# First attention, second set of eight heads: exponentials read PSUM one head at a time, with the negated row maximum as bias, and 1/4 goes into the head mask

## The chip, the cores and the metric

The kernel runs on one core of a Trainium2 chip. A time is the device time of one execution, in microseconds (us), lower being better. The core has five engines with queues of their own: TensorE (PE, with its weight loads PEld), VectorE (DVE), ScalarE (ACT), GpSimd (POOL) and SyncE (SP, which here only starts transfers).

## The reference

A two-layer network on x of 16 batches x 128 tokens x 256 features: cross attention, a quantised FFN, an mLSTM-like attention, and a mixture of eight experts. The change lies in the first part:

```python
qp = q @ Wq                       # q: layer norm of x
kp, vp = split(kv @ Wkv)          # kv: the context
# 16 heads of 16 features, scale = 16 ** -0.5 = 1/4
dots = jnp.einsum('bhid,bhjd->bhij', qh, kh) * scale
attn = jax.nn.softmax(dots, axis=-1)
out = jnp.einsum('bhij,bhjd->bhid', attn, vh)
x = x + out.reshape(B, N, D) @ Wout
```

## The kernel before

Each engine has a program of its own, written out by hand, and they meet at semaphores: `x.then_inc(s, 1)` raises s when x is done, `engine.wait_ge(s, n)` holds the engine's queue until s is n. Each queue runs strictly in its order.

The first attention handles one batch (128 tokens, 16 heads) per step, 16 steps, b = 0 to 15. The heads are worked in two sets of eight, m = 0 and 1; the scores of a set, 128 x 1024 fp32, fill two PSUM banks, `S_ps[m]`. In a step, for each set:

- TensorE makes the scores (`scores`, L698). A query tile of 32 features holds two heads; GpSimd has multiplied the keys with a 0/1 mask, `pair_mask`, so that each head meets only its own features (`mask_k`, L522, into `kbd`).
- VectorE takes the maximum over each row of each head (L1304, into `row_max`) and subtracts it from all of the scores, PSUM to SBUF (L1306, into `probs`): `softmax_shift`.
- ScalarE takes the exponential of `probs` in place, 1024 columns in one instruction, with 1/4 as scale (L1033): `exps`.
- TensorE transposes the eight heads back into the same PSUM banks (`probs_transposes`, L705); ScalarE copies them to SBUF (`probsT_copy`, L1041); TensorE multiplies with the values (`values`, L718), which carry a column of ones, so that the sum of the exponentials comes out beside them.

Between these, the engines work on the step before (`tail_a` L725, `tail_norm` L1313 and L1315, `tail_b` L731, ScalarE's copy L1058, `tail_c` L737, the output product, and VectorE's `tail_add`, L1320 and on) and on the step after (`front_transposes`, `front_products` L682 and L687, ScalarE's copies L1025, L1029, L1037). TensorE's order in a step is:

```python
scores(b, p, 0); values(b - 1, 1 - p, 1); front_transposes(b + 1, ...)
scores(b, p, 1); tail_a(b - 1); front_products(b + 1, ...); tail_b(b - 1)
probs_transposes(b, 0); tail_c(b - 1); probs_transposes(b, 1); values(b, p, 0)
```

ScalarE's order: outT_copy, front, `exps(b, 0)`, qk_copy, v_copy, the copy of L1058, `exps(b, 1)`, probsT_copy twice. VectorE's order: softmax_shift(b, 0), norm, tail_norm, softmax_shift(b, 1), tail_add; and in the last seven steps a piece of the FFN's weight preparation behind that (`late`: gate_up_maxima in step 9, then weight_scales, down_rounded, gate_up_scaled, gate_up_shifted, gate_up_rounded, early_norms).

Before the loop VectorE takes the statistics of the 16 batches in groups of four (L1271 to L1275), GpSimd raises each group to -1/2 (L513), and only behind the fourth does GpSimd's queue come to the first mask products. `pair_mask` itself is made by VectorE after the first group, from `head_mask`.

Of the kernel before, what the change touches and what calls it, by code (L numbers as in the profile page):

```python
# [8 lines left out]
def build(nc, x, ctx_in, wq, wkv, wout, clip_x, clip_down, w_gate, w_up, w_down, ig_k, ig_b, fg_k, fg_b, rms_scale,  # L9
# [5 lines left out]
    ALU = mybir.AluOpType  # L15
    ACT = mybir.ActivationFunctionType
    AX = mybir.AxisListType

    B, S, D = x.shape
    P = 128  # L20
    KT = D // P
    H0 = 16
    DH0 = D // H0
    HT = P // DH0
# [27 lines left out]
    with stack:  # L52
        def sb(name, shape, dt=F32):
            return stack.enter_context(nc.sbuf_tensor(name, shape, dt))
# [4 lines left out]
        def sem(name):  # L59
            return stack.enter_context(nc.semaphore(name))  # L60
# [24 lines left out]
        pair_mask = sb("pair_mask", [P, 2])  # L85
# [112 lines left out]
        def bank(n, *shape, count=1, dt=F32):  # L198
            view = psum[:, n, :] if count == 1 else psum[:, n:n + count, :].rearrange("p n c -> p (n c)")
            if dt != F32:  # L200
                view = view.bitcast(dt)
            names = "abcde"[:len(shape)]
            return view.rearrange(f"p ({' '.join(names)}) -> p {' '.join(names)}", **dict(zip(names[1:], shape[1:])))
# [4 lines left out]
        S_ps = [bank(3, HT, P, count=2), bank(5, HT, P, count=2)]  # L208
# [7 lines left out]
        consts_ready = sem("consts_ready")  # L216
# [13 lines left out]
        max_ready = sem("max_ready")  # L230
        shifted_ready = sem("shifted_ready")
        probs_ready = sem("probs_ready")
# [257 lines left out]
        def _(pool):  # L490
# [25 lines left out]
            def mask_k(b, p, inner=False):  # L516
                pool.wait_ge(qk_evac, b + 1)
                if inner or b >= 2:

                    pool.wait_ge(s_done, 2 * (b - 2) + 2)  # L520
                for m in range(KT):
                    nc.gpsimd.tensor_tensor(kbd[:, p, m, :, :],  # L522
                                            qkT[:, p, KT + m, :].unsqueeze(1).to_broadcast([P, 2, P]),
                                            pair_mask[:].unsqueeze(2).to_broadcast([P, 2, P]),
                                            ALU.mult).then_inc(kbd_ready, 1)
# [2 lines left out]
            nc.gpsimd.memset(one_col[:], 1.0).then_inc(fw_preset, 1)  # L528
            nc.gpsimd.tensor_copy(ident_b[:], ident[:]).then_inc(fw_preset, 1)

            pool.wait_ge(consts_ready, 7)
            mask_k(0, 0)
            mask_k(1, 1)
            with pool.Fori(0, (B - 2) // 2) as i:
# [485 lines left out]
        def _(act):  # L1020
            act_fn = nc.scalar.activation
# [7 lines left out]
                act_fn(qkT[:, p, :, :], bank1[:, :, :], ACT.Copy).then_inc(qk_evac, 1)  # L1029

            def exps(b, m):
                act.wait_ge(shifted_ready, 2 * b + m + 1)
                act_fn(probs[:, m, :, :], probs[:, m, :, :], ACT.Exp, scale=float(DH0) ** -0.5).then_inc(probs_ready, 1)  # L1033

            def v_copy(b, p):
                act.wait_ge(v_done, b + 1)
# [39 lines left out]
            for q in range(3):  # L1076
                last = act_fn(wguT[:, :, 4 * q:4 * q + 4, :].rearrange("p k n c -> p n k c"), bank(q, 4, KT, P, dt=BF16), ACT.Copy)
# [190 lines left out]
        def _(dve):  # L1268
            def row_stats(b, chain):

                nc.vector.bn_stats(stats[:, 0, :], x_sb[:, b, :]).then_inc(ln_chain, 1)  # L1271
                dve.wait_ge(ln_chain, chain + 1)
                nc.vector.bn_aggr(mv[:, b, :], stats[:, 0, :]).then_inc(ln_chain, 1)
                dve.wait_ge(ln_chain, chain + 2)
                nc.vector.tensor_scalar_add(rstd[:, b:b + 1], mv[:, b, 1:2], LN_EPS).then_inc(ln_chain, 1)  # L1275

            def norm(b, p, inner=False):
                if inner or b >= 2:

                    dve.wait_ge(t1_done, b - 1)  # L1280
                nc.vector.tensor_scalar(xn[:, p, :], x_sb[:, b, :], mv[:, b, 0:1], rstd[:, bass.ds(b, 1)] if inner else rstd[:, b:b + 1],
                                        ALU.subtract, ALU.mult).then_inc(xn_ready, 1)
# [6 lines left out]
            for i in range(4):  # L1289
                dve.wait_ge(x_loaded[i], 16)  # L1290
                for b in range(4 * i, 4 * i + 4):
                    row_stats(b, 3 * b)
                if i == 0:
                    dve.wait_ge(rstd1_ready, 1)
                    norm(0, 0)
                    norm(1, 1)
                    dve.wait_ge(consts_ready, 6)
                    nc.vector.tensor_reduce(pair_mask[:], head_mask[:].rearrange("p (g r) -> p r g", r=2), AX.X,
                                            ALU.add).then_inc(consts_ready, 1)
            dve.wait_ge(rstd1_ready, 4)  # L1300

            def softmax_shift(b, m):
                dve.wait_ge(s_done, 2 * b + m + 1)
                nc.vector.tensor_reduce(row_max[:, m, :], S_ps[m][:, :, :], AX.X, ALU.max).then_inc(max_ready, 1)  # L1304
                dve.wait_ge(max_ready, 2 * b + m + 1)
                nc.vector.tensor_tensor(probs[:, m, :, :], S_ps[m][:, :, :],  # L1306
                                        row_max[:, m, :].unsqueeze(2).to_broadcast([P, HT, P]),
                                        ALU.subtract).then_inc(shifted_ready, 1)

            def tail_norm(b):  # L1310
                dve.wait_ge(to_done, b + 1)
# [247 lines left out]
            for n in range(2):  # L1559
                last = nc.vector.tensor_scalar(gates8[0:R, n, :], gates8[0:R, n, :], gbias[0:R, n:n + 1], None, ALU.add)  # L1560
# [289 lines left out]
```

## Time and profile before

| | |
|---|---|
| three runs | 877.24, 881.13, 881.49 us, median 881.13 |
| the profiled execution | 880.42 us, its span 878.7 us |
| busy over the span | PE 686.7, PEld 473.8, DVE 545.8, ACT 394.6, POOL 248.4 us |
| granted TensorE clock, mean | 0.867 |
| subtractions of L1306 | 32, 1224 ns each |
| maxima of L1304 | 32, 1219 ns each |
| exponentials of L1033 | 32, 1057 ns each |

The span goes from the first to the last instruction; the time of the execution has 1.7 us around it. Busy time is that of each engine alone, over all stages; the first attention takes some 180 us of the span, and only its rows bear on the change. The granted clock is a share of TensorE's full speed, 1.00 being the higher level and 0.50 the lower.

### The profile page before, as it was taken

The page shows a single profiled execution, that of the slowest core. Times are in us where ns is not written, and L with a number is a line of the kernel's source. Part 1 is how long each engine was busy: PE and PEld are TensorE (multiplying, and loading weights), DVE is VectorE, ACT ScalarE, POOL GpSimd, SP SyncE. Part 2 cuts the span into 40 slices and gives each one's busy share as a digit, 9 for nine tenths or more (in the row PEclk, how much of TensorE's full clock was granted, in tenths as well). Part 3 has the DMA queues.
Part 4 walks back from the last instruction along what each step waited for, and adds up shares of the span by engine and source line. Part 5 has one row for each costly group of instructions (what it writes and reads, how often), then busy time and mean ns, then how long its engine had stood idle before and what let it go on. Part 6 is the DMA issues. An engine that isn't in the chain of part 4 may idle for free.

```text
span 878.7 us, 19300 instructions
## 1 busy us (share of the span) xinstructions
PE 686.7 (78%) x4567; PEld 473.8 (54%) x4611; DVE 545.8 (62%) x1394; ACT 394.6 (45%) x811; POOL 248.4 (28%) x372
## 2 busy tenths in 40 slices
PE   3999999983745695277616989898989989889992
PEld 2778877761223473266513556565655655556661
DVE  5577789974989654398785464555455455564440
ACT  1466655544633254355314453535444545453330
POOL 3111111110000200644402353545344272653421
PEclk9799999985985598555556999999999999999996
DMA  8100000000000111511172433343251515431113
GB/s 256 31 13 14 15 12 12 0 1 0 1 0 0 31 54 30 211 31 30 41 248 66 127 73 87 104 125 73 37 160 24 167 30 166 127 72 24 30 25 108
DMA packets 45843, 58.41 MB, mean 66 GB/s; under 512 B 13496, under 2 KB 39416, under 8 KB 45272
## 3 DMA queue, kind: packets, MB, share of 16 engines
q1 hardware_dynamic: 38328, 47.79, 16.7%
q0 software_dynamic: 7488, 10.31, 7.4%
q8 instruction: 11, 0.18, 0.1%
q14 instruction: 16, 0.13, 0.0%
HBM read 145.90 MB, written 11.80 MB: 179 GB/s over the span
## 4 chain that ended last, share of the span: by engine, by line
PE 47%; DVE 20%; issue 15%; POOL 7%; DMA 3%; ACT 3%; DVEq 2%; ACTq 1%; POOLq 1%; SPq 0%
PE psum L962 16%; PE psum L984 7%; PE psum L698 3%; PE psum L975 3%; PE psum L682 3%; PE psum L705 2%; POOL region L638 2%; PE psum L862 2%; DVE region L1455 2%; PE psum L718 1%; PE psum L737 1%; DMA region<-xrow_dram,next_token 1%; PE psum L687 1%; PE psum L855 1%; POOL region L561 1%
## 5 line engine op out<-in xcount | busy, mean ns | idle before, releaser
L962 PE MATMUL psum<-region 128*128 x897 | 209.3, 381 | 18.9 <-issue 6.0
L962 PEld LDWEIGHTS psum<-region 128*128 128x128 bf16 x936 | 91.7, 98 | 117.8 <-issue 28.6
L984 PE MATMUL psum<-region 128*128 x936 | 113.9, 280 | 6.3 <-DVE region L1799 3.7
L984 PEld LDWEIGHTS psum<-region 128*128 128x128 bf16 x936 | 92.1, 100 | 23.1 <-issue 9.7
L1769 DVE TENSOR_TENSOR region<-psum,region 128x512 f32<-128x512 f32 x78 | 53.9, 691 | 72.8 <-ACT region L1209 63.5
L1209 ACT ACTIVATE region<-psum 128x512 f32<-128x512 f32 x78 | 46.5, 597 | 116.6 <-PE psum L962 108.2
L620 POOL DMA_INDIRECT sum_dram<-region,tok_idx x39 | 62.0, 1589 | 6.9 <-issue 6.6
L608 POOL TENSOR_TENSOR pause_p<-minus_half 128x1 f32<-128x1 f32 x37 | 7.1, 193 | 192.3 <-DVE next_token L1785 191.6
L1230 ACT ACTIVATE pause_a<-one_col 128x1 f32<-128x1 f32 x117 | 23.7, 202 | 83.9 <-issue 68.8
L1799 DVE TENSOR_TENSOR region<-psum,region 128x1024 bf16<-128x1024 f32 x39 | 47.7, 1222 | 19.1 <-ACT region L1217 19.1
L522 POOL TENSOR_TENSOR region<-region,pair_mask 128x256 f32<-128x256 f32 x32 | 18.9, 613 | 138.3 <-ACT region L1029 138.3
L609 POOL DMA_INDIRECT region<-xrow_dram,next_token x39 | 41.0, 1052 | 39.6 <-DVE next_token L1764 27.4
L1749 DVE MEMSET pause_d<- 128x1 f32 x80 | 4.7, 59 | 73.4 <-ACT pause_a L1233 39.1
L1304 DVE TENSOR_REDUCE region<-psum 128x8 f32<-128x1024 f32 x32 | 39.0, 1219 | 14.6 <-PE psum L698 14.5
L1217 ACT ACTIVATE region<-psum 128x1024 bf16<-128x1024 f32 x39 | 39.9, 1023 | 16.0 <-PE psum L975 15.0
L1232 ACT ACTIVATE region<-region 128x2048 f32 x24 | 45.8, 1909 | 0.0
L895 PE MATMUL psum<-region 128*128 128x96 f32 x128 | 32.0, 433 | 17.6 <-DVE region L1579 8.8
L1033 ACT ACTIVATE region<-region 128x1024 f32<-128x1024 f32 x32 | 33.8, 1057 | 25.8 <-DVE region L1306 25.8
L1751 DVE TENSOR_TENSOR region<-region 128x2048 f32 x17 | 39.0, 2294 | 2.6 <-issue 2.6
L698 PE MATMUL psum<-region 32*128 32x256 f32 x256 | 38.1, 417 | 3.0 <-POOL region L522 3.0
L975 PEld LDWEIGHTS psum<-ident,region 128*128 128x128 f32 x312 | 36.5, 141 | 7.4
L975 PE MATMUL psum<-ident,region 128*128 128x128 f32 x312 | 40.4, 273 | 0.0
(295 smaller groups left out, 1362.6 us busy)
## 6 DMA issues: line engine op xcount, KB each, us to landing
region<-in_L_ffn_w SPq DMA_DIRECT2D x117, 1024.0 KB
region<-in_ctx SPq DMA_DIRECT2D x48, 128.0 KB, 2.1
region<-neg_max_dram SPq DMA_DIRECT2D x4, 1024.0 KB, 7.6
xrow_dram<-region SPq DMA_DIRECT2D x1, 2080.0 KB, 7.8
x_sb<-in_x SPq DMA_DIRECT2D x4, 512.0 KB, 6.6
sum_dram<-x_sb SPq DMA_DIRECT2D x1, 2048.0 KB, 7.5
region<-in_L_ffn_w_down SPq DMA_DIRECT2D x1, 704.0 KB, 8.3
region<-in_L_ffn_w_gate SPq DMA_DIRECT2D x1, 640.0 KB, 8.9
```

Of the source, the lines that this page charges most:

```text
L609: pool.indirect_dma_start(xg[:, p, :], None, xrow_dram, bass.IndirectOffsetOnAxis(ap=next_token[:, p:p + 1], axis=0)).then_inc(xg_loaded[p ...
L620: pool.indirect_dma_start(sum_dram, bass.IndirectOffsetOnAxis(ap=tok_idx[:, p:p + 1], axis=0), y_d[:, p, :], None, compute_op=ALU.add).the ...
L698: last = mm(S_ps[s][:, 4 * r + 2 * m:4 * r + 2 * m + 2, :], qkT[rows, p, m, :], kbd[rows, p, m, :, :], start=True, stop=True)
L962: last = mm(psum[:, 2 * f + n, :], (xT_lo if xl else xT_hi)[:, p, k, :], weights_at(place, wl, n, k * F1 + f * FH, FH), start=(i == 0), st ...
L975: last = tr(bank(4, F1 // P, P, count=2)[:, f, :], h_d[:, p, f * P:(f + 1) * P], ident[:])
L984: last = mm(psum[:, 7, 0:D], (hT_lo if hl else hT_hi)[:, f, :], weights_at(place, wl, 2, f * D, D), start=(i == 0), stop=(i == 3 * (F1 // ...
L1209: act_fn(sil_d[:, f, :], psum[:, 2 * f, :], ACT.Silu).then_inc(sil_d_ready, 1)
L1217: act_fn(hT_hi, bank(4, F1 // P, P, count=2), ACT.Copy).then_inc(hT_high, 1)
L1232: act_fn(expert_w[:, bass.ds(place + n * PART, PART)], stage[:, p, n, :], ACT.Copy)
L1304: nc.vector.tensor_reduce(row_max[:, m, :], S_ps[m][:, :, :], AX.X, ALU.max).then_inc(max_ready, 1)
L1769: tt(h_d[:, p, f * FH:(f + 1) * FH], psum[:, 2 * f + 1, :], sil_d[:, f, :], ALU.mult).then_inc(h_d_ready, 1)
L1799: tt(hT_lo, bank(4, F1 // P, P, count=2), hT_hi, ALU.subtract).then_inc(hT_low, 1)
```

## The change

For the second set of heads (m = 1) the subtraction on VectorE is gone. The maximum is written negated, and ScalarE waits for it and takes eight exponentials of 128 columns, one per head, that read the scores in PSUM and take that head's negated maximum as bias. The first set keeps subtraction (now an addition of the negated maximum) and its one exponential. The scale 1/4 leaves the exponentials: `pair_mask` is multiplied with it once, so that the scores come out scaled; that multiply raises `consts_ready` to 8, for which GpSimd now waits.

```diff
--- before.py
+++ after.py
@@ -528,7 +528,7 @@
             nc.gpsimd.memset(one_col[:], 1.0).then_inc(fw_preset, 1)
             nc.gpsimd.tensor_copy(ident_b[:], ident[:]).then_inc(fw_preset, 1)
 
-            pool.wait_ge(consts_ready, 7)
+            pool.wait_ge(consts_ready, 8)
             mask_k(0, 0)
             mask_k(1, 1)
             with pool.Fori(0, (B - 2) // 2) as i:
@@ -1029,8 +1029,14 @@
                 act_fn(qkT[:, p, :, :], bank1[:, :, :], ACT.Copy).then_inc(qk_evac, 1)
 
             def exps(b, m):
-                act.wait_ge(shifted_ready, 2 * b + m + 1)
-                act_fn(probs[:, m, :, :], probs[:, m, :, :], ACT.Exp, scale=float(DH0) ** -0.5).then_inc(probs_ready, 1)
+                if m == 0:
+                    act.wait_ge(shifted_ready, b + 1)
+                    act_fn(probs[:, m, :, :], probs[:, m, :, :], ACT.Exp).then_inc(probs_ready, 1)
+                else:
+                    act.wait_ge(max_ready, 2 * b + 2)
+                    for h in range(HT):
+                        last = act_fn(probs[:, m, h, :], S_ps[m][:, h, :], ACT.Exp, bias=row_max[:, m, h:h + 1])
+                    last.then_inc(probs_ready, 1)
 
             def v_copy(b, p):
                 act.wait_ge(v_done, b + 1)
@@ -1297,15 +1303,18 @@
                     dve.wait_ge(consts_ready, 6)
                     nc.vector.tensor_reduce(pair_mask[:], head_mask[:].rearrange("p (g r) -> p r g", r=2), AX.X,
                                             ALU.add).then_inc(consts_ready, 1)
+                    dve.wait_ge(consts_ready, 7)
+                    nc.vector.tensor_scalar_mul(pair_mask[:], pair_mask[:], float(DH0) ** -0.5).then_inc(consts_ready, 1)
             dve.wait_ge(rstd1_ready, 4)
 
             def softmax_shift(b, m):
                 dve.wait_ge(s_done, 2 * b + m + 1)
-                nc.vector.tensor_reduce(row_max[:, m, :], S_ps[m][:, :, :], AX.X, ALU.max).then_inc(max_ready, 1)
-                dve.wait_ge(max_ready, 2 * b + m + 1)
-                nc.vector.tensor_tensor(probs[:, m, :, :], S_ps[m][:, :, :],
-                                        row_max[:, m, :].unsqueeze(2).to_broadcast([P, HT, P]),
-                                        ALU.subtract).then_inc(shifted_ready, 1)
+                nc.vector.tensor_reduce(row_max[:, m, :], S_ps[m][:, :, :], AX.X, ALU.max, negate=True).then_inc(max_ready, 1)
+                if m == 0:
+                    dve.wait_ge(max_ready, 2 * b + 1)
+                    nc.vector.tensor_tensor(probs[:, m, :, :], S_ps[m][:, :, :],
+                                            row_max[:, m, :].unsqueeze(2).to_broadcast([P, HT, P]),
+                                            ALU.add).then_inc(shifted_ready, 1)
 
             def tail_norm(b):
                 dve.wait_ge(to_done, b + 1)
```

ScalarE's instructions of one step inside the loop, in the order of its queue, first as they were (from the copy L1045 that opens the step):

```order
L1045 ACTIVATE region<-psum 128x512
L1024 REGISTER_ALU
L1025 ACTIVATE region<-psum 128x512
L1032 ISA
L1033 ACTIVATE region<-region 128x1024
L1029 ACTIVATE region<-psum 128x512
L1037 ACTIVATE region<-psum 128x16x16
L1058 ACTIVATE region<-psum 128x256
L1032 REGISTER_ALU
L1033 ACTIVATE region<-region 128x1024
L1041 ACTIVATE region<-psum 128x1024 x2
```

and with the change (line numbers shift; L1034 is the exponential of set 0, L1038 those of set 1, L1064 the copy before them):

```order
L1051 ACTIVATE region<-psum 128x512
L1024 REGISTER_ALU
L1025 ACTIVATE region<-psum 128x512
L1033 REGISTER_ALU
L1034 ACTIVATE region<-region 128x1024
L1029 ACTIVATE region<-psum 128x512
L1043 ACTIVATE region<-psum 128x16x16
L1063 REGISTER_ALU
L1064 ACTIVATE region<-psum 128x256
L1036 ISA
L1038 ACTIVATE region<-psum,region 128x128 x8
```

In the place of one 128x1024 activation on SBUF stand eight of 128x128 that read PSUM; nothing else of the step has moved.

VectorE's instructions in the middle of the same step, from the maximum of set 0 to the residual add, as they were:

```order
L1303 ISA
L1304 TENSOR_REDUCE region<-psum 128x8
L1306 TENSOR_TENSOR region<-psum,region 128x1024
L1281 ISA x2
L1281 TENSOR_SCALAR region<-x_sb,mv,rstd 128x256
L1313 RECIPROCAL region<-psum 128x16
L1315 TENSOR_TENSOR region<-psum,region 128x256
L1303 REGISTER_ALU
L1304 TENSOR_REDUCE region<-psum 128x8
L1306 TENSOR_TENSOR region<-psum,region 128x1024
L1320 ISA
L1320 TENSOR_TENSOR x_sb<-x_sb,psum 128x256
```

and with the change:

```order
L1311 ISA
L1312 TENSOR_REDUCE region<-psum 128x8
L1315 TENSOR_TENSOR region<-psum,region 128x1024
L1287 ISA x2
L1287 TENSOR_SCALAR region<-x_sb,mv,rstd 128x256
L1322 RECIPROCAL region<-psum 128x16
L1324 TENSOR_TENSOR region<-psum,region 128x256
L1311 REGISTER_ALU
L1312 TENSOR_REDUCE region<-psum 128x8
L1329 ISA
L1329 TENSOR_TENSOR x_sb<-x_sb,psum 128x256
```

The second TENSOR_TENSOR of 128x1024 is gone, and the residual add (L1329, before L1320) follows the second maximum directly.

## Rows read from the trace of the kernel before

**Rows 1.** The windows view: busy us and instructions of each engine, TensorE clock, transfers.

```profile
63.00:73.00 10.00, 10.00 (x101) 8.17 (x100) 7.69 (x16) 6.42 (x10) 1.18 (x2) 1.00 0.04 13
123.00:135.00 12.00, 10.15 (x97) 7.65 (x96) 11.65 (x23) 5.85 (x10) 1.18 (x2) 1.00 0.04 11
178.00:189.00 11.00, 8.42 (x75) 6.41 (x73) 9.28 (x18) 4.97 (x7) 2.27 (x1) 0.80 0.01 1
```

**Rows 2.** The chain that ended last, first attention: start us, us, what.

```profile
32.85 1.09 PE psum L705 x8
...
112.64 0.87 PE psum L705 x8
...
121.74 0.88 PE psum L737 x4
...
124.60 3.26 DVE w_amax L1363
```

**Rows 3.** Timeline of step 5: start us, us, engine, line, operation [idle before].

```profile
78.88 1.21 DVE L1304 TENSOR_REDUCE region<-psum 128x8 f32<-128x1024 f32 x1
...
80.13 1.23 DVE L1306 TENSOR_TENSOR region<-psum,region 128x1024 f32<-128x1024 f32 x1
...
81.18 0.38 ACT L1058 ACTIVATE region<-psum 128x256 f32<-128x256 f32 x1
81.44 1.06 ACT L1033 ACTIVATE region<-region 128x1024 f32<-128x1024 f32 x1
...
81.79 1.03 PE L737 MATMUL psum<-region 128*128 128x256 f32 x4
...
82.65 1.04 PE L705 MATMUL psum<-ident,region 128*128 128x128 f32 x8
...
83.62 0.65 PE L718 MATMUL psum<-region 128*32 128x128 f32 x16
```

**Rows 4.** ScalarE's groups by shape: count, busy us, mean ns, idle before.

```profile
L1033 ACT ACTIVATE region<-region 128x1024 f32<-128x1024 f32 x32 | 33.8, 1057 | 25.8 <-DVE region L1306 25.8
L1041 ACT ACTIVATE region<-psum 128x1024 f32<-128x1024 f32 x32 | 32.7, 1022 | 6.1 <-PE psum L705 6.1
...
L1105 ACT ACTIVATE sil<-psum,gu_scale 128x512 f32<-128x512 f32 x24 | 16.4, 686 | 12.8 <-DVE region L1455 12.8
...
L1158 ACT ACTIVATE region<-region 128x128 f32 x40 | 12.9, 390 | 2.0 <-issue 1.6
...
L1029 ACT ACTIVATE region<-psum 128x512 f32<-128x512 f32 x16 | 9.5, 594 | 20.2 <-PE psum L682 20.2
...
L1037 ACT ACTIVATE region<-psum 128x256 f32<-128x256 f32 x16 | 6.1, 383 | 4.5 <-PE psum L687 4.5
```

**Rows 5.** Timeline of ScalarE alone, in the later mLSTM stage.

```profile
385.50 0.37 ACT L1174 ACTIVATE region<-psum 128x256 f32<-128x256 f32 x1
385.76 0.41 ACT L1175 ACTIVATE region<-region 128x256 f32 x1
...
386.37 1.28 ACT L1158 ACTIVATE region<-region 128x128 f32 x4
```

**Rows 6.** Timeline of step 10.

```profile
131.11 1.21 DVE L1304 TENSOR_REDUCE region<-psum 128x8 f32<-128x1024 f32 x1
...
131.25 0.44 PE L731 MATMUL psum<-ident,region 128*128 128x128 f32 x2 [0.67 <-DVE region L1315]
...
132.36 1.23 DVE L1306 TENSOR_TENSOR region<-psum,region 128x1024 f32<-128x1024 f32 x1
...
133.62 1.06 ACT L1033 ACTIVATE region<-region 128x1024 f32<-128x1024 f32 x1 [1.25 <-DVE region L1306]
...
134.73 1.09 PE L705 MATMUL psum<-ident,region 128*128 128x128 f32 x8 [1.18 <-ACT region L1033]
```

**Rows 7.** Timeline of the start, GpSimd.

```profile
18.53 1.01 POOL L513 TENSOR_TENSOR rstd<-rstd,minus_half 128x4 f32<-128x4 f32 x1 [1.95 <-DVE rstd L1275]
```

**Rows 8.** Timeline of step 15, TensorE's output product.

```profile
187.55 1.91 PE L737 MATMUL psum<-region 128*128 128x256 f32 x4
```

## The prediction

> **What bounds the kernel now.** The change touches only the first attention, which runs from about 21 to 200 us of the span, so I read that stretch alone. First the windows [rows 1]: between 63 and 73 us TensorE is busy 10.00 us of 10 at clock 1.00, VectorE 7.69, ScalarE 6.42. Between 123 and 135 us it is VectorE that is full, 11.65 us of 12, and TensorE has gaps. So the sixteen steps of the loop have two regimes. The chain that ended last says where they part [rows 2]: the transposes of the second set of heads (L705) stand on it once per step from 32.85 us, in step 0, to 112.64 us, in step 8, that is nine times; from step 9 it leaves TensorE after the output product (L737, 121.74 us), takes VectorE's tail of the step and goes into the FFN weight preparation that is hung on the last seven steps (`late`), first the 3.26 us piece of w_amax at 124.60. I call steps 0 to 8 TensorE's steps and steps 9 to 15 VectorE's steps.
>
> Then the timeline of one TensorE step, step 5 [rows 3], which decides the case. The row maximum of set 1 is there from 78.88 + 1.21 = 80.09. VectorE subtracts it (80.13, 1.23 us). But ScalarE doesn't wait for that subtraction: it starts the exponentials at 81.44, right behind its two copies, and they end at 82.50. TensorE's second transposes start at 82.65, 0.86 us after the product before them (81.79), which is that product's own pace. So the exponentials of set 1 come out 0.1 us or so before TensorE wants them, and their start is set by ScalarE's queue, not by VectorE. Nothing there waits for the subtraction, and whatever lengthens the exponentials is paid by TensorE.
>
> **The change part by part.** (1) VectorE loses one 128x1024 subtraction (1.23 us) in each of 16 steps, 19.7 us of busy time. In the nine TensorE steps that is worth nothing, as just read. In the seven others it takes the place of a link that the exponentials have to wait for; see (3). The edits that cost nothing: `negate` on the maximum and the missing scale on the exponentials change no instruction's size; the 1/4 is in the mask, and the mask products (L522) keep their shape.
>
> (2) ScalarE's one exponential of 1024 columns (1.06 us, SBUF to SBUF) becomes eight of 128 columns that read PSUM and take a bias from SBUF. That form is not in the trace, so I bound it by its neighbours [rows 4]. A copy from PSUM takes 0.594 us for 512 columns and 0.383 for 256, so 128 take 0.383 - 0.106 = 0.277. An operand by pointer costs 0.686 - 0.594 = 0.09 (the silu of L1105, with its scale column, against the plain copy of 512 columns). Sum 0.367. The other way: the decays (L1158) are just this instruction but for SBUF as source, 0.390 us; PSUM as source is 0.035 faster (1.057 against 1.022 for 1024 columns), so 0.355. I take 0.36. What counts more is the distance from start to start in a run of them. Four decays in a row take 1.28 us [rows 5], (1.28 - 0.39) / 3 = 0.298 apart; less 0.035 for PSUM that is 0.263. A PSUM copy of 256 columns starts the next instruction 0.26 us later, for 0.37 of its own [rows 5], an overlap of 0.11, and 0.367 - 0.11 = 0.257. I take 0.26. Eight then take 7 x 0.26 + 0.36 = 2.18 us in place of 1.06.
>
> The high bound is the decays' own pace, 7 x 0.298 + 0.39 = 2.48 us. The low bound leaves the pointer free: 7 x (0.277 - 0.11) + 0.277 = 1.45 us. I stay near the high side since the decays are the nearest row.
>
> The Trainium skill, page "ScalarE: Activation LUTs", section "What ACT_TABLE_LOAD costs", gives an activation with a bias by pointer 280 ns + 0.833 ns a column, and an overlap of 93 ns back to back. By that rule eight would be 7 x 0.294 + 0.387 = 2.44 us, and the total below would be about +12.3 us instead of +9.9; the decays' rows agree with it (0.390 and 0.298), and it makes no difference for a source in PSUM, where the copies' rows do.
>
> In step 5 the exponentials start at 81.44 as before (the maximum was ready at 80.09, before ScalarE's copy of L1058 began at 81.18), and end at 83.62. Where TensorE has waited for them, its transposes start 0.05 us after their end and take 1.09 instead of 1.04 [rows 3, 6], so everything behind starts (83.62 + 0.05 + 0.05) - 82.65 = 1.07 us later. All that follows in the step hangs on those transposes or on ScalarE's copies behind the same exponentials (the values at 83.62), which keep their distance: ScalarE's probsT copy ends about 0.1 us before the eight transposes do, as now. The next step's exponentials start again behind TensorE's L687 and ScalarE's two copies, so nothing is caught up and the delay adds up: nine steps, 9 x 1.07 = 9.6 us; a step grows from 9.97 us (the first and the last L705 of [rows 2] are 79.79 us apart, over 8 steps) to 11.0.
>
> (3) VectorE's steps. In step 10 [rows 6] the maximum of set 1 ends at 132.32, the subtraction at 133.59, the exponential at 134.68, and TensorE waits until 134.73, idle meanwhile. With the change the eight exponentials can start at 132.36 and end at 134.54: -0.14 us. The subtraction that goes and the longer exponentials pay for each other, there and in steps 12, 13 and 15. VectorE isn't released sooner either: its next work there, the residual add, waits for TensorE's L737 (132.42 + 1.13 = 133.55), just when the subtraction ends now. In steps 9, 11 and 14 the exponentials are off the chain, because it goes from L737 through VectorE; but there TensorE starts the following step 1.07 us later and had only 0.5 to 0.7 us of idle before its next link with VectorE (0.67 in step 10 [rows 6]), so 0.3 to 0.4 us comes through. I put the seven steps at 0 in all, -1 to +1.
>
> (4) The start. VectorE gets a wait for its own mask reduction and a small multiply, about 0.2 us with the semaphore, ahead of twelve batches' statistics. GpSimd's fourth rsqrt waits for these, and the first mask product and first scores for that [rows 7]: +0.2 us. The new `consts_ready` count of 8 is long reached by then.
>
> **Sum.** 9.6 + 0 + 0.2 = +9.8. The later stages hold none of the changed lines. The profiled execution took 880.42 us (span 878.7); the three runs' median is 881.13, 0.7 above. 881.1 + 9.8 = 890.9, from the profiled execution 890.2.
>
> **Rivals.**
> A, forecast: the exponentials become TensorE's wait in nine steps. With the bounds of (2): run 2.48 gives 1.37 per step, +12.5; run 1.9 gives 0.79, +7.3; with +-1 for (3): 887 to 895. Chance 0.80.
>
> B, not slower: the pointer is hidden when the instructions stand back to back. Run 1.45: (1.45 - 1.11) = 0.34 per step, 3.1 + 0.2, less about 0.7 in each of steps 10, 13 and 15: +1.2, 882.3. Below a run of 1.11 us a TensorE step costs nothing, and that is where it turns; if the eight followed at the pace of their columns alone (7 x 0.106 + 0.36 = 1.10), VectorE's three steps would gain 1.2 us each: 877.7. For it: the first of the bounds is only argued. Against it: the decays, four in a row, show 0.298 and not 0.106. Chance 0.07, of which 0.02 for a gain over 0.5%.
>
> C, the clock: TensorE now idles 1.1 us in nine more steps. At the end of this stage, where VectorE kept it waiting, the granted clock is 0.80 over a stretch [rows 1], the lower level (1.2 GHz) for part of it, and the product of L737, 1.03 us in step 5, took 1.91 [rows 3, 8]. If it fell for some 7 to 10 us in the loop, 3 to 5 us would come on top: 895 to 897. Against it: in 123 to 135 us TensorE was idle 1.85 us and the clock stayed at 1.00 [rows 1], at its higher level (2.4 GHz). Chance 0.08.
>
> D, more hangs on the second set than I see: the eight reads of PSUM slow beside TensorE's transposes into the other banks, or the run is no better than one duration each, 8 x 0.37 = 2.96. Then 1.85 per step: +17, 898. Chance 0.05.
>
> **The numbers.** Likeliest 890.9. The range goes from the low side of A, with a little of B, to the low side of C, with the other stages' scatter of +-2 us that the three runs show: 885.5 to 896.5. A measurement of this kernel tells about 0.5%, 4.4 us, from no change. Faster 0.02 and within it 0.08 are B and the lowest end of A; slower 0.90.
>
> **What would show it.** In the profile after: eight exponentials, 0.36 us each, taking about 2.2 us together; TensorE's L705 waiting some 1.1 us for them in steps 0 to 8, step length 11.0; VectorE's busy time down by some 19.5 us and the span up all the same; the first scores 0.2 us later; clock 1.00 through the loop. The forecast is wrong if the run takes under 1.6 us, or if a TensorE step doesn't stretch by what the run grew.

## The result, and the profile after

The changed kernel is slower: median 892.81 us of four runs against 880.10 of the kernel before, ratio 1.0142, 95% interval 1.0105 to 1.0178. Timed a second time, as the last of the experiments, it took 890.17 against 879.26, ratio 1.0133 (1.0114 to 1.0152). The forecast was 890.9 with a range of 885.5 to 896.5. The profiled execution took 889.77 us, span 888.0.

From the page of the changed kernel, busy time by engine and the granted clock in 40 slices:

```profile
PE 678.4 (76%) x4567; PEld 466.2 (52%) x4611; DVE 527.3 (59%) x1379; ACT 412.1 (46%) x923; POOL 251.0 (28%) x372
...
PEclk9899999997997599555555999999999999999997
```

VectorE is busy 18.5 us less than before (545.8), ScalarE 17.5 us more (394.6), and the span is 9.3 us longer. The load moved from one engine to the other, almost one for one; below it turns out that only the second one counts. What the two instructions became, in the groups of ScalarE and of VectorE (the latter for 20 to 215 us):

```profile
L1038 ACT ACTIVATE region<-psum,region 128x128 f32<-128x128 f32 x128 | 34.8, 396 | 0.2 <-DVE region L1312 0.2
L1047 ACT ACTIVATE region<-psum 128x1024 f32<-128x1024 f32 x32 | 33.8, 1057 | 4.3 <-PE psum L705 4.3
```

```profile
L1312 DVE TENSOR_REDUCE region<-psum 128x8 f32<-128x1024 f32 x32 | 39.0, 1218 | 24.1 <-PE psum L698 24.0
L1315 DVE TENSOR_TENSOR region<-psum,region 128x1024 f32<-128x1024 f32 x16 | 19.6, 1224 | 0.5
```

L1038 is the new line, 128 times, 0.396 us each; L1047, the copy of the transposed heads, is L1041 of before; sixteen subtractions are left (L1315) of 32. The windows that answer to [rows 1], moved to the same work. The first starts with the residual add of step 3 and spans one step, 11.0 us now; the second starts 0.36 us behind the residual add of step 9, as 123.00 did before:

```profile
65.51:76.51 11.00, 10.15 (x98) 8.05 (x98) 6.47 (x14) 7.46 (x17) 1.18 (x2) 1.00 0.04 12
131.91:143.91 12.00, 10.57 (x102) 8.48 (x103) 10.37 (x22) 8.22 (x19) 1.18 (x2) 1.00 0.03 11
```

In a TensorE step VectorE has fallen from 7.69 to 6.47 us, by one subtraction. TensorE was busy 10.00 us of ten and is busy 10.15 of eleven: it now waits. Its clock stays at 1.00. In the stretch of step 9 to 10, where VectorE was full (11.65 of 12), it is busy 10.37 of 12, and TensorE isn't full either (10.57). The timeline of step 5 shows the wait; the columns are those of [rows 3]:

```profile
83.52 1.21 DVE L1312 TENSOR_REDUCE region<-psum 128x8 f32<-128x1024 f32 x1
...
85.82 0.38 ACT L1064 ACTIVATE region<-psum 128x256 f32<-128x256 f32 x1
86.08 2.17 ACT L1038 ACTIVATE region<-psum,region 128x128 f32<-128x128 f32 x8
...
86.43 1.03 PE L737 MATMUL psum<-region 128*128 128x256 f32 x4
87.60 0.42 DVE L1329 TENSOR_TENSOR x_sb<-x_sb,psum 128x256 f32 x1 [2.88 <-PE psum L737]
...
88.07 1.09 ACT L1047 ACTIVATE region<-psum 128x1024 f32<-128x1024 f32 x1
...
88.31 1.09 PE L705 MATMUL psum<-ident,region 128*128 128x128 f32 x8 [0.85 <-ACT region L1038]
...
89.33 0.65 PE L718 MATMUL psum<-region 128*32 128x128 f32 x16
```

The maximum is ready at 84.73, ScalarE's copy L1064 starts at 85.82, and the eight exponentials start at 86.08, 0.26 us behind it, just as the one of 1024 columns did. They take 2.17 us where that took 1.06. TensorE's product L737 starts at 86.43; its transposes could follow 0.86 us later, at 87.29, and start at 88.31, 0.06 us behind the exponentials. VectorE meanwhile idles 2.88 us before the residual add L1329. ScalarE's copy of the transposed heads (L1047), which starts right behind the run, shows 1.09 instead of 1.02 us, and the values (L718) follow 1.02 us after L705's start, where it was 0.97 [rows 3]: the 0.05 us that the forecast had counted for transposes that had to wait. The chain that ended last now has the exponentials on it in each of the first nine steps:

```profile
33.23 1.09 PE psum L705 x8
...
42.03 2.15 ACT region L1038 x8
...
121.33 1.09 PE psum L705 x8
...
130.64 0.88 PE psum L737 x4
...
133.50 3.26 DVE w_amax L1372
...
141.53 1.92 ACT region L1038 x7
143.49 1.09 PE psum L705 x8
```

Compare [rows 2]: there the transposes followed TensorE's own product. Now each L705 stands behind some 2.16 us of L1038. From 130.64 to 133.50 the chain goes through VectorE as before, and comes back through L1038 at 141.53. That is step 10, the counterpart of [rows 6]:

```profile
140.01 1.21 DVE L1312 TENSOR_REDUCE region<-psum 128x8 f32<-128x1024 f32 x1
...
141.26 2.17 ACT L1038 ACTIVATE region<-psum,region 128x128 f32<-128x128 f32 x8
...
141.48 1.03 PE L737 MATMUL psum<-region 128*128 128x256 f32 x4
142.54 0.42 DVE L1329 TENSOR_TENSOR x_sb<-x_sb,psum 128x256 f32<-128x256 f32 x1 [1.32 <-PE psum L737]
```

The exponentials start at 141.26, 0.04 us behind the maximum, and end at 143.43: 2.21 us after the maximum, where subtraction and exponential took 2.36. VectorE, spared its subtraction, idles 1.32 us for L737.

Starts of VectorE's residual add, one per step, give the length of each step without reading anything else. The first one stands in step 1, ahead of that step's second transposes, so the first distance holds what step 1 pays, and the fifteenth what step 15 pays. The fifteen distances, in us:

| kernel | first eight | ninth to thirteenth | fourteenth, fifteenth |
|---|---|---|---|
| before | 9.93 to 9.98, 9.85 at the end; sum 79.49 | 10.95, 11.36, 10.81, 11.35, 10.93 | 11.46, 9.28 |
| changed | 10.99 to 11.05, 10.92 at the end; sum 88.03 | 10.99, 11.16, 11.00, 11.04, 11.11 | 9.74, 9.28 |

Eight steps give 8.54 us, 1.07 each. The next five are 55.40 and 55.30. The 11.46 of the kernel before is not its softmax: the clock stood at its lower level from 184.6 to 191.4 us in that execution, and in other profiles of the same steps it did or didn't (below), so 1.7 us of the real difference are hidden in this pair of profiles.

### The profile page after: what moved, and what is told of

Same layout as the page of the kernel before. It is cut to its first block, busy times and chain, and to the rows that moved or that the text cites. A ratio compares the mean times of both kernels' runs of the same rounds, so it can differ in the third digit from the quotient of the medians.

```text
span 888.0 us, 19411 instructions
## 1 busy us (share of the span) xinstructions
PE 678.4 (76%) x4567; PEld 466.2 (52%) x4611; DVE 527.3 (59%) x1379; ACT 412.1 (46%) x923; POOL 251.0 (28%) x372
## 4 chain that ended last, share of the span: by engine, by line
PE 44%; DVE 18%; issue 15%; POOL 8%; ACT 6%; DMA 3%; DVEq 2%; POOLq 1%; ACTq 1%; SPq 0%
PE psum L962 16%; PE psum L984 6%; PE psum L698 3%; POOL region L638 3%; ACT region L1038 3%; PE psum L682 3%; PE psum L975 3%; DVE region L1464 2%; PE psum L862 2%; PE psum L705 2%; PE psum L718 2%; PE psum L687 1%; PE psum L855 1%; POOL region L561 1%; POOL pause_p L636 1%
## 5 line engine op out<-in xcount | busy, mean ns | idle before, releaser
L962 PE MATMUL psum<-region 128*128 x897 | 210.3, 383 | 21.1 <-POOL pause_p L640 7.4
L962 PEld LDWEIGHTS psum<-region 128*128 128x128 bf16 x936 | 91.9, 98 | 120.6 <-issue 32.0
L984 PE MATMUL psum<-region 128*128 x936 | 109.1, 273 | 6.2 <-DVE region L1808 3.8
L984 PEld LDWEIGHTS psum<-region 128*128 128x128 bf16 x936 | 89.4, 98 | 21.0 <-issue 9.7
L705 PE MATMUL psum<-ident,region 128*128 128x128 f32 x256 | 34.1, 276 | 14.8 <-ACT region L1038 14.7
L975 PE MATMUL psum<-ident,region 128*128 128x128 f32 x312 | 40.4, 273 | 0.0
L975 PEld LDWEIGHTS psum<-ident,region 128*128 128x128 f32 x312 | 36.5, 141 | 7.4
L705 PEld LDWEIGHTS psum<-ident,region 128*128 128x128 f32 x256 | 28.2, 141 | 21.3 <-ACT region L1038 21.0
```

Source lines behind the costliest of these rows:

```text
L705: last = tr(S_ps[m][:, h, :], probs[:, m, h, :], ident[:])
L962: last = mm(psum[:, 2 * f + n, :], (xT_lo if xl else xT_hi)[:, p, k, :], weights_at(place, wl, n, k * F1 + f * FH, FH), start=(i == 0), st ...
L975: last = tr(bank(4, F1 // P, P, count=2)[:, f, :], h_d[:, p, f * P:(f + 1) * P], ident[:])
L984: last = mm(psum[:, 7, 0:D], (hT_lo if hl else hT_hi)[:, f, :], weights_at(place, wl, 2, f * D, D), start=(i == 0), stop=(i == 3 * (F1 // ...
```

## The experiments

Theory A is the forecast: ScalarE's queue stands before TensorE's second transposes, its eight exponentials take 1.1 us longer than the one, and nine steps pay. The rivals: M, the loss comes from the mask, the start or later stages; V, VectorE's relief is worth something that the loop's loss hides; and on the price, whether it is the cutting into eight, the pointer, or the work on ScalarE as such that costs. Ratios are to the kernel before, on the same chip each time.

### The mask alone

```diff
-                if m == 0:
-                    act.wait_ge(shifted_ready, b + 1)
...
-                        last = act_fn(probs[:, m, h, :], S_ps[m][:, h, :], ACT.Exp, bias=row_max[:, m, h:h + 1])
...
+                act.wait_ge(shifted_ready, 2 * b + m + 1)
+                act_fn(probs[:, m, :, :], probs[:, m, :, :], ACT.Exp).then_inc(probs_ready, 1)
```

and the subtraction for both sets; the 1/4 stays in the mask.

> Only the mask part of the change: 1/4 in the head mask, negated maxima, but both sets keep VectorE's subtraction and the one exponential of 1024 columns. If the loss is TensorE's wait for the eight exponentials (theory A), this is as fast as before, the start aside: 0 to +0.3 us in the attention, ratio 0.998 to 1.003 to the kernel before. If the loss came from the start, the mask or from later stages that merely run in another phase (rival M), it would show here: +3 us or more.

Measured 880.37 against 879.45, ratio 1.0013 (0.9999 to 1.0027). Its timeline, ScalarE in step 6:

```profile
90.56 0.38 ACT L1058 ACTIVATE region<-psum 128x256 f32<-128x256 f32 x1
90.83 1.06 ACT L1033 ACTIVATE region<-region 128x1024 f32<-128x1024 f32 x1
91.78 1.02 ACT L1041 ACTIVATE region<-psum 128x1024 f32<-128x1024 f32 x1
```

The exponential starts 0.27 us behind the copy and takes 1.06 us, as before; the first eight steps sum to 79.47 us, then 10.95, 11.36, 10.80, 11.35, 10.94, 9.75, 9.28. The mask and the start cost about 1 us by the medians, between nothing and 2.4 us by the interval. This kernel is also the better base for comparing steps, its profile having no lower clock in the last two distances: against it the changed kernel's fifteen distances sum to 162.35 - 153.90 = +8.45 us.

### Eight exponentials, SBUF to SBUF, without a bias

```diff
-                act_fn(probs[:, m, :, :], probs[:, m, :, :], ACT.Exp)
+                    for h in range(HT):
+                        last = act_fn(probs[:, m, h, :], probs[:, m, h, :], ACT.Exp)
```

for m = 1, on top of the mask-only kernel.

> As the mask-only kernel, but the exponential of set 1 is cut into eight of 128 columns, SBUF to SBUF, behind VectorE's subtraction, without a bias by pointer. Theory A with the pointer as most of the price: starts 0.2 us apart (0.298 less 0.09), a run of about 1.7 us, TensorE 0.6 us late per step in nine steps, in all +5 to +6 us; VectorE's steps are longer too, since the subtraction stays. If it is the cutting itself that costs (the pointer being free), the run is as long as with bias, some 2.2 to 2.4 us, and the kernel +10 us or more.

Measured ratio 1.0112 (1.0063 to 1.0161), 888.79 against 879.45 or +9.3 us, more than the +5 to +6 expected. The group of the eight, then step 5 in the timeline:

```profile
L1037 ACT ACTIVATE region<-region 128x128 f32<-128x128 f32 x128 | 27.2, 302 | 4.0 <-DVE region L1313 4.0
```

```profile
84.53 1.70 ACT L1037 ACTIVATE region<-region 128x128 f32<-128x128 f32 x8
...
86.28 1.09 PE L705 MATMUL psum<-ident,region 128*128 128x128 f32 x8 [0.37 <-ACT region L1037]
```

The run takes 1.70 us, just as expected, and steps are 10.52 us, +0.59. That makes 4.7 us in eight steps. The last seven sum to 4.2 us more than in the mask-only kernel. There the exponentials still stand behind the subtraction, and in steps 10, 12 and 15 both are on the chain: steps of 12.03 and 13.54 us are among them (11.36 and 11.35 there). The clock has a part in it that isn't told apart here: it stood at its lower level from 163.8 to 167.2 us, in the second of these steps, and from 194.5 to 201.3, in the last two. The expectation had put too little on these seven.

### Eight exponentials from PSUM, without a bias

```diff
-                        last = act_fn(probs[:, m, h, :], S_ps[m][:, h, :], ACT.Exp, bias=row_max[:, m, h:h + 1])
+                        last = act_fn(probs[:, m, h, :], S_ps[m][:, h, :], ACT.Exp)
```

> The changed kernel with the bias left out of the eight exponentials of set 1: they still wait for the maximum and read PSUM, but nothing is subtracted, so the guard against large scores is missing in that set. Theory A with the pointer price: starts about 0.17 apart, run 1.45 us, TensorE 0.35 us late per step, +3 us over before in the loop and about -1 in VectorE's steps: +1 to +3 us. If the pointer is free back to back, the run stays at 2.17 us and the kernel at +9 to +13.

Measured ratio 1.0044 (1.0027 to 1.0062), 884.02 against 879.45, +4.6 us: the run and the step came out as expected, the whole above the +1 to +3. Its fifteen distances sum to 2.9 us more than those of the mask-only kernel, with the clock at its lower level from 187.2 to 190.6 us in one of them; the rest isn't traced.

```profile
L1038 ACT ACTIVATE region<-psum 128x128 f32<-128x128 f32 x128 | 23.5, 325 | 0.2 <-DVE region L1312 0.2
```

```profile
93.52 1.48 ACT L1038 ACTIVATE region<-psum 128x128 f32<-128x128 f32 x8
...
95.05 1.09 PE L705 MATMUL psum<-ident,region 128*128 128x128 f32 x8 [0.15 <-ACT region L1038]
```

A run of 1.48 us (1.45 expected), steps of 10.30 to 10.41 (10.23 at the end), +0.37. With these two the price of the pieces is measured: starts are (1.48 - 0.325) / 7 = 0.165 us apart from PSUM without a pointer, (1.70 - 0.302) / 7 = 0.200 from SBUF, and (2.17 - 0.396) / 7 = 0.253 from PSUM with the bias by pointer. And TensorE's delay follows the run with one constant:

| set 1's exponentials | run, us | step, us | step over 9.93 | run less 1.11 |
|---|---|---|---|---|
| one of 1024, from SBUF | 1.06 | 9.93 | 0 | below 0 |
| eight, PSUM, no bias | 1.48 | 10.30 | 0.37 | 0.37 |
| eight, SBUF, no bias | 1.70 | 10.52 | 0.59 | 0.59 |
| eight, PSUM, bias | 2.17 | 11.00 | 1.07 | 1.06 |

### The change in steps 9 to 15 only, and in steps 0 to 8 only

```diff
+                new = isinstance(b, int) and b >= 9
-                if m == 0:
+                if m == 0 or not new:
```

with the same condition in VectorE's softmax_shift, and, for the other kernel, the opposite condition in both. Both programs' loops cover steps 1 to 8, and steps 9 to 15 are written out.

> The change made in steps 9 to 15 alone, where VectorE is the bound; steps 0 to 8 keep subtraction and one exponential for set 1 (1/4 in the mask throughout). Theory A: the seven steps come out at 0, -1 to +1 us; ratio 0.998 to 1.002. Rival V (VectorE's relief is real there and the loop's loss was larger than it looks): -2 us or more. If the exponentials cost in every step alike, +7 us.

Measured ratio 1.0004 (0.9987 to 1.0021). Steps 9.93 to 9.98, then 11.00, 11.16, 11.00, 11.04, 11.11, 9.74, 9.29: the changed kernel's last seven behind the old kernel's first nine.

> The counterpart of the kernel with the change in steps 9 to 15 alone: the change in steps 0 to 8, and subtraction plus one exponential for set 1 in steps 9 to 15. Theory A: the whole loss is here, nine steps of 1.09 us, 9.8 us, of which the whole changed kernel keeps all: +9 to +13 us, ratio 1.010 to 1.014, like the whole change. A rival in which the two halves act on each other (the later steps' relief pays back part) would make this slower than the whole change by 2 us or more.

Measured ratio 1.0103 (1.0075 to 1.0131), 884.89 against 875.73, +9.2 us. Steps of 11.0, then 10.95, 11.37, 10.79, 11.36, 10.93. The loss is in the first nine steps, all of it; rival V falls, for the last seven give nothing back by themselves.

### One exponential from PSUM, without a bias

```diff
-                    for h in range(HT):
-                        last = act_fn(probs[:, m, h, :], S_ps[m][:, h, :], ACT.Exp, bias=row_max[:, m, h:h + 1])
-                    last.then_inc(probs_ready, 1)
+                    act_fn(probs[:, m, :, :], S_ps[m][:, :, :], ACT.Exp).then_inc(probs_ready, 1)
```

> The changed kernel with one exponential of 1024 columns straight from PSUM in place of the eight, without a bias, so nothing is subtracted in set 1 (the maximum is still taken and waited for): VectorE's relief without the longer run. Theory A: run 1.02 us, TensorE's steps back at 9.93 us, and in VectorE's steps the subtraction is gone from the chain: -2 to -4 us against before. If VectorE's subtraction was worth nothing anywhere, the time is that of before.

Measured ratio 0.9991 (0.9974 to 1.0007), from 2.3 us faster to 0.6 slower: a miss, no gain that can be told. The steps are at 9.93 again, and of the later ones 10.95, 10.07, 10.81, 10.96, 10.03, 11.05, 9.29: the second, fourth and fifth became shorter, by 2.6 us in all against the mask-only kernel, and the sixth longer by 1.3, its clock at the lower level from 182.9 us on. So even with a short exponential VectorE's relief of 1.2 us in each of seven steps is worth 2.6 us in this profile, and the whole doesn't confirm that much. In the first and the third of these steps nothing changed (10.95 and 10.81): they are held by the chain from TensorE's product to the weight preparation [rows 2], on which the subtraction of set 1 doesn't lie.

### Five heads ahead of the copies

```diff
                 exps(b, 0)
+                early = 5 if inner or b == 0 else 0
+                if early:
+                    exps(b, 1, range(early))
...
-                exps(b, 1)
+                exps(b, 1, range(early, HT))
...
                 softmax_shift(b, 0)
+                first = inner or b == 0
+                if first:
+                    softmax_shift(b, 1)
...
                     tail_norm(b - 1)
-                softmax_shift(b, 1)
+                if not first:
+                    softmax_shift(b, 1)
```

> The changed kernel with the same instructions in another order in steps 0 to 8: VectorE takes the maximum of set 1 right behind the subtraction of set 0, and ScalarE puts five of the eight exponentials ahead of its copies, into the time in which it idled 1.0 us for TensorE; three stay behind the copies. Steps 9 to 15 as in the changed kernel. Theory A (what costs is how much of the run stands behind the last copy, 3 x 0.27 + 0.1 us): steps of 9.9 us again, total -1 to +1 us against before, 9 to 12 us faster than the changed kernel. If it is ScalarE's total work, or its reads of PSUM beside TensorE's writes, that slow the step, the loss stays at +8 us or more.

Measured ratio 1.0020 (1.0002 to 1.0037), 877.14 against 875.73, +1.4 us: a little above the expected -1 to +1, and close to what the mask alone showed. The same instructions as in the changed kernel, and 9.93 to 9.98 us a step:

```profile
86.26 1.22 DVE L1322 TENSOR_REDUCE region<-psum 128x8 f32<-128x1024 f32 x1
...
86.38 1.06 ACT L1034 ACTIVATE region<-region 128x1024 f32<-128x1024 f32 x1 [0.77 <-DVE region L1325]
...
87.51 1.40 ACT L1039 ACTIVATE region<-psum,region 128x128 f32<-128x128 f32 x5
...
88.78 0.62 ACT L1029 ACTIVATE region<-psum 128x512 f32<-128x512 f32 x1
...
89.59 0.38 ACT L1069 ACTIVATE region<-psum 128x256 f32<-128x256 f32 x1
89.86 0.89 ACT L1039 ACTIVATE region<-psum,region 128x128 f32<-128x128 f32 x3
...
90.20 1.03 PE L737 MATMUL psum<-region 128*128 128x256 f32 x4
...
91.07 1.04 PE L705 MATMUL psum<-ident,region 128*128 128x128 f32 x8
```

The maximum, now behind the subtraction of set 0, starts at 86.26; five exponentials run from 87.51 to 88.91, in ScalarE's pause before the copies, three from 89.86 to 90.75. L705 starts at 91.07, 0.87 us behind L737's start at 90.20, without a wait. ScalarE's work is the same as in the changed kernel, and it reads PSUM as often, at about the same pace (one takes 0.38 us in the mean: (1.40 - 0.38) / 4 = 0.26 us from start to start in the five, (0.89 - 0.38) / 2 = 0.26 in the three), while TensorE works on; the loss is gone all the same. So the price of the change is neither: it is how much of the run stands between ScalarE's last copy and TensorE's transposes.

### No maximum at all

```diff
+                act.wait_ge(s_done, 2 * b + m + 1)
+                act_fn(probs[:, m, :, :], S_ps[m][:, :, :], ACT.Exp).then_inc(probs_ready, 1)
```

for both sets, and both calls of softmax_shift gone. Neither set's scores are shifted, which leaves the guard against large scores out.

> Neither set takes a maximum or subtracts; ScalarE takes one exponential of 1024 columns per set straight from the scores in PSUM. The guard against large scores is left out. VectorE loses 4.9 us a step. Theory A: TensorE's steps stay at 9.93 us, for VectorE wasn't on their chain; all of the gain comes from the last seven steps, which become TensorE's steps too: -6 to -10 us against before. If VectorE's queue also held the first nine, the gain would be 15 us or more.

Measured ratio 0.9908 (0.9881 to 0.9934), 866.70 against 875.73. Steps of 9.85 to 9.97 from the first to the thirteenth. VectorE lost 4.9 us a step and the first eight steps sum to 79.46 us, to 0.03 what they did before: its softmax was never on their chain. The last seven steps sum to 66.71 us against 74.43 in the mask-only kernel, 7.7 of the 9.0 us gained; the other 1.3 aren't placed.

### The weight preparation spread over steps 2 to 12

The last result says that VectorE's load costs some 8 us in steps 9 to 15 and nothing before. What those steps have more than the others is the weight preparation. So that work was spread instead, in eleven pieces, ahead of the residual add: once with the softmax as it was, once with the changed softmax, five heads first up to step 13.

```diff
-            rest = (gate_up_maxima, weight_scales, down_rounded, gate_up_scaled, gate_up_shifted, gate_up_rounded, early_norms)
+            mids = {2: lambda: gate_up_maxima(0), 3: lambda: gate_up_maxima(1), 4: down_maxima, 5: weight_scales,
+                    6: down_scaled, 7: down_shifted, 8: down_rounded, 9: lambda: gate_up_scaled(0),
+                    10: lambda: gate_up_scaled(1), 11: gate_up_shifted, 12: gate_up_rounded}
...
                 softmax_shift(b, 1)
+                if mid:
+                    mid()
                 if inner or b >= 1:
                     tail_add(b - 1)
```

> The kernel before, its softmax untouched, with VectorE's FFN weight preparation cut into pieces of at most 1.8 us and laid over steps 2 to 12, ahead of the residual add, where VectorE idles 1.6 us for TensorE's product; early_norms stays in step 15. If VectorE's load binds steps 9 to 14 only because all of the preparation hangs there, those steps fall back from 10.8-11.4 to about 10.0 us: -5 to -8 us, with no change to the exponentials at all. If VectorE is bound by its sum, nothing moves.

> The changed kernel with five heads' exponentials ahead of the copies, the maximum of set 1 early, in steps 0 to 13, and the weight preparation laid over steps 2 to 12 as in the other kernel. VectorE has 2.9 us of room where each piece goes. Theory A: steps of 9.9 us everywhere up to 13: -6 to -9 us against before, level with the other spread kernel or 1 to 2 us ahead of it, since its pieces of 1.6 to 1.8 us leave that one no room. If it is no better than the other, the change has nothing to give even in its best place.

Softmax of before: 873.08 against 879.26, ratio 0.9933 (0.9916 to 0.9949). Changed softmax with five heads first: 872.76, ratio 0.9924 (0.9907 to 0.9942). Both beat both kernels; between them nothing can be told. The windows of the first and of the second:

```profile
63.00:73.00 10.00, 10.00 (x100) 8.17 (x99) 9.27 (x17) 6.42 (x10) 1.26 (x3) 1.00 0.05 13
123.00:135.00 12.00, 11.62 (x116) 9.40 (x118) 11.30 (x29) 7.85 (x12) 1.28 (x2) 1.00 0.04 11
```

```profile
63.00:73.00 10.00, 10.00 (x101) 8.20 (x100) 7.85 (x15) 7.46 (x17) 1.18 (x2) 1.00 0.04 13
123.00:135.00 12.00, 12.00 (x128) 9.52 (x125) 9.87 (x28) 8.51 (x18) 1.25 (x2) 1.00 0.04 11
```

VectorE at 9.27 us of ten and 11.30 of twelve in the one, 7.85 and 9.87 in the other; TensorE full in both but for 0.38 us. The changed softmax's relief is there to see, in the eighth to the eleventh distance (10.42, 10.19, 10.03, 10.32 in the one, 10.03, 9.93, 9.96, 9.86 in the other, 1.2 us together). Two pieces there took 2.01 us each, more than the 1.8 us meant. But all fifteen distances sum to 147.75 and 147.80 us. The second kernel loses in step 14 what it had gained, 9.22 us against 8.14, for in that step its eight exponentials stand behind the copies again, and TensorE waits:

```profile
173.23 1.09 PE L705 MATMUL psum<-ident,region 128*128 128x128 f32 x8 [0.85 <-ACT region L1039]
```

So this was not quite the best place for the change. With step 14 in the other order too it might be 1 us ahead, an estimate from the 1.08 us between 9.22 and 8.14; no run shows it.

### The changed kernel once more

> The changed kernel once more, to see whether the 12.7 us between the medians belong to it, when its attention took 9 us more in the profile. Theory A: the attention's 8.5 to 9.5 us and nothing systematic behind it: ratio 1.009 to 1.013. If the later stages lose something too (rival M), 1.014 or more again.

Ratio 1.0133 (1.0114 to 1.0152), between what theory A and what rival M asked for, so it doesn't decide. Steps of 11.00 to 11.06, 10.93 at the end of the eight. In this execution the clock fell late in the attention (193.4 to 196.8 us), and the fourteenth distance is 11.07 and not 9.74.

## Why the prediction was right

**What bounds a TensorE step.** As forecast: the exponentials' start is set by ScalarE's queue, not by VectorE. Their distance to the copy before them is 0.26 us in [rows 3] and in the changed kernel, and taking VectorE's whole softmax away changes the step by nothing. The wait of L705 that the profile shows is 0.85 us and not 1.1, since L737 before it is drawn with 1.03 us where the next start comes 0.86 behind; from that pace the transposes are 1.02 us late.

**The run of eight.** Forecast 0.36 us each, 0.26 apart, 2.18 together; measured 0.396, 0.253 and 2.17. A single one is longer than worked out (0.325 without bias where the slope of the copies gave 0.277), and they overlap more; the two errors cancel. The rule of the Trainium skill ("ScalarE: Activation LUTs", "What ACT_TABLE_LOAD costs"), 280 ns + 0.833 ns a column with a bias by pointer and an overlap of 93 ns, makes it 2.44 us, an estimate that is too long here: it has 0.294 from start to start, and this run from PSUM shows 0.253. The Trainium skill's price of a pointer, about 93 ns, is close: (2.17 - 1.48) / 8 = 0.086 us here. (The totals named beside that rule, +12.3 instead of +9.9, should be +12.2 instead of +9.8 by the forecast's own sum.)

**The delay.** Forecast 1.07 us per step, measured 1.07. The experiments with runs of 1.48 and 1.70 us lie on the same line, so the point from which rival B would have held, a run of 1.11 us, is confirmed by two more lengths of the run.

**Steps 9 to 15.** Forecast 0 in all, measured 74.32 against 74.43 us in the mask-only kernel, -0.1, and by itself a ratio of 1.0004. The sum is partly luck. Forecast were -0.14 us in each of steps 10, 12, 13 and 15 and +0.3 to +0.4 in each of 9, 11 and 14, which adds up to about +0.5 and was put at 0. Measured against the mask-only kernel, steps 9 to 15 have +0.04, -0.20, +0.20, -0.31, +0.17, -0.01 and 0.00: steps 10 and 12 gained and 11 lost as forecast, but 13 lost where a gain was expected, and 9 and 14 came out even. What I didn't say is how evenly they come out: the old steps alternate between 10.8 and 11.4, the new steps 9 to 13 are all 11.0 to 11.2. The exponentials now hold TensorE in each of the seven (idle 0.85 to 0.98 us before L705), where before only some did (10, 12 and 13 of steps 9 to 13).

**The start.** Forecast 0.2 us. The first scores start at 21.17 us in the kernel before, 21.85 and 21.20 in the changed kernel's two profiles, and anywhere from 21.26 to 22.64 in the other kernels with the same mask; the profiles can't tell 0.2 us there. Step 0's own share of about 1 us is not seen alone either, as the clock comes up at different times in it (31.0 us before, 29.8 after).

**The sum.** 9.6 + 0.2 = 9.8 was forecast. The attention has 8.45 us from the first residual add to the last, and step 0 on top, if it pays what the others do; that is 9.5, close to the forecast. The medians differ by 12.7 and by 10.9 us, and the narrower of the two intervals, 1.0114 to 1.0152, is 10.0 to 13.4 us: the forecast difference of 9.8 lies just below its low end, and near the low end of the first, which is 9.2 to 15.7. That 890.9 is only 1.9 us from 892.81 owes 1 us to the base, 881.1, since the kernel before came to 880.10 in the end. Between the medians 1 to 3 us are therefore not accounted for. The stretch behind the last residual add was 679.9 us before and 682.1 and 680.7 in the changed kernel's profiles, but 680.5 to 681.0 in three kernels that measured level or nearly so (mask only, late steps only, five heads first), and 675.5 to 683.5 over all, on different chips, so no profile shows where they would be. The three level kernels' own ratios, 1.0013, 1.0004 and 1.0020, leave room for about 1 us of mask and start. The rest stays open, and with it the part of rival M that puts a small loss into the later stages.

**The rivals.** B fell with the first run of 2.17 us. C: the clock stayed at 1.00 in the loop, even with TensorE idle 0.85 us in every step. D: nothing more hangs on the second set than the transposes and what follows them, as the five-heads-first kernel shows.

## What to carry to other kernels

Work moved from a fuller engine to an emptier one is judged by where it lands in the second one's queue, not by either one's share: ScalarE was busy 64% of the step and had pauses of 1.0 us, but the eight exponentials went behind its last copy, just ahead of what TensorE waits for. Before an instruction is cut into pieces, price the distance from start to start and add up the run; then look for a pause in which part of it fits. And when a relief gives nothing where it was made, ask what the relieved engine is late with: here the weight preparation was hung on seven steps, and spreading it gave 6 us without touching the softmax.

## What the runs showed of the hardware

- ScalarE, 128 columns of 128 partitions: an exponential in a run of eight starts 0.165 us after the one before when it reads PSUM, 0.200 from SBUF, 0.253 from PSUM with its bias by pointer. Yet in such runs one from PSUM shows a longer duration (0.325 us) than one from SBUF (0.302), and eight times 0.325 is 2.60 us where the run took 1.48: in a run the durations shown don't give its length.
- TensorE's granted clock at the end of the attention differed between profiles of kernels that do the same there: lower level (1.2 GHz) from 184.6 to 191.4 us in the kernel before, from 193.4 to 196.8 in one profile of the changed kernel, not at all in the other or in the mask-only kernel. It is worth 1.3 to 1.7 us in one step, which is more than several of the effects studied here; a comparison step by step has to leave that step out.
